# Layer-1 mixer of a graph transformer kernel: chunks of two tiles, with the feed-forward part of one chunk beside the attention of the next

## The chip, the cores and the metric

The kernel runs on one core of a Trainium2 chip. The metric is the device time of one execution in microseconds, the median of three runs. A core has five engines that run their own instruction streams in order: TensorE (PE in the profile; PEld is its weight load), VectorE (DVE), ScalarE (ACT), GpSimd (POOL) and SyncE (SP). They wait for one another by semaphores.

## The reference

Two layers on 3125 nodes with 256 features. Each adds a graph part and a mixer part, and then a feed-forward part with experts. The change touches only the place where layer 1 computes its graph part and its mixer:

```python
xn = _layernorm(x, axis=-1)
x = x + _L1_gnn_ref(xn, edge_index, ...) + _L1_mix_ref(xn[None], ...)[0]

# _L1_gnn_ref: graph attention over 50000 edges, 2 heads of 128
Wh = (x @ W_w + W_b).reshape(N, H, D)
e = leaky_relu(s[src] + t[dst])
ex = exp(e - segment_max(e, src)[src])
agg = segment_sum(ex / denom[src] * Wh[dst], src)

# _L1_mix_ref: linear attention with 8 heads of 32, then a feed-forward part of width 1024
q_phi, k_phi = _phi(x @ Wq + bq), _phi(x @ Wk + bk)
kv = einsum('blhd,blhe->bhde', k_phi, v);  k_sum = k_phi.sum(axis=1)
z = 1.0 / (einsum('blhd,bhd->blh', q_phi, k_sum) + 1e-06)
out = einsum('blhd,bhde,blh->blhe', q_phi, kv, z) @ Wo + bo
x = _layernorm(x + out, ln1_g, ln1_b)
ff = relu(x @ W1 + b1) @ W2 + b2
x = _layernorm(x + ff, ln2_g, ln2_b)
```

## The kernel before

The nodes lie in 25 tiles of 125 rows. `program` (L2983) runs one stage after another, each a `Block` with an instruction stream per engine, and a barrier of all engines stands between two stages. The change touches one stage, `sums_and_mix1` (L2577). Two streams of work without data in common run side by side in it.

The **edge stream** is the weighted sum over the edges. There are 25 groups of 16 columns. For a group t, POOL gathers 16 times 128 rows of `wh_dram` into one of four buffers `he_buf` (L2616); a buffer is free for group t+4 when the DMA that stores group t into `he_result` has landed (SP, L2634). DVE makes the exponents (`logits`, from L2777) and sets `e_ready`; ACT takes the exponential (`weights`, L2700) and multiplies each of the 16 columns in place (`weigh`, L2708, two instructions a column); DVE adds each column to the one after it (L2801 to L2819, 15 long instructions in a chain), copies the last (L2825), and sets `summed`, upon which SP stores the group.

The **mixer stream** is the attention and the feed-forward part. It first makes the key tables of all nodes (`keys_tensor`, `keys_scalar`, `keys_vector`), and then goes through the nodes in six chunks of four tiles (500 columns) and a last one of one tile. In a chunk each step needs the one before it:

- PE: query product (L2648, banks 0 and 1); ACT: positive and negative part and exponential (L2720 to L2724), sets `q_phi`.
- PE: `kv` and `ks` products (L2655 to L2658, banks 2, 3, 0, 1), sets `o_made`; DVE: `attention`, which adds, takes the reciprocal (L2857) and multiplies (L2860), sets `o_ready`.
- PE: output product for each tile (L2664 to L2667: bias row, residual through the identity, two of `wo`; banks 4 to 7), sets `o_made2`; DVE: sums of the first layer norm (L2836 to L2841), sets `var1`; ACT: square root (L2744), sets `std1`; DVE: normalization (L2845, L2848) into `y`, sets `y_ready`.
- PE: eight transposes (L2672, banks 0 and 1); ACT: scale and shift into `yT` (L2729), sets `y_moved`.
- PE: up product, eight blocks f of 128 hidden features (L2679, banks 0 to 3); ACT: relu of each (L2714), sets `acted`; PE: down product for each tile (L2685 to L2690, banks 4 to 7), sets `f_made` per tile; DVE: sums of the second layer norm; ACT: square root (L2761); DVE: normalization, times `norm2`, plus `norm2`, added to `X` (L2872 to L2877).

Nothing schedules this: the order of each stream is written out by hand. DVE's order in a chunk is `logits(t+1)`, `sums(t)`, `attention`, `logits(t+2)`, the first half of `sums(t+1)`, `after_attention`, the rest of `sums(t+1)`, `logits` and `sums` of the next two groups, `after_feed_forward`. ACT puts the relus between the columns of `weigh(t+3)`. PE has nothing but the mixer, one chunk behind the other. The room of the hidden features `hT` also holds the queries and the attention output (`qr`, `ql`, `oT`), and the tables of the keys before them. Where a name in the trace is `m_hT`, it is one of these.

## Time and profile before

| | us |
|---|---|
| median of three runs | 3766.0 (3750.4 to 3766.4) |
| the profiled execution | 3773.5 |
| its span, first to last instruction | 3771.8 |
| of it the stretch from the first `logits` to the last addition into `X` | 642.7 |
| PE busy in the whole span | 2309.4 |
| DVE busy in the whole span | 1909.2 |
| ACT busy in the whole span | 1335.4 |
| POOL busy in the whole span | 1332.4 |

No engine is busy for most of the span, since the stages have different limits. What a change in one stage is worth is read from that stage: from who waits for whom in it, and from the instructions in order of time. In the rows below, times are microseconds from the start of the span unless they are marked ns. An `x` with a number is a count of records; a matrix product in 32-bit floats leaves two records, one transpose leaves one. "DVEq" or "ACTq" as the releaser is a semaphore set by that engine's queue after a drain.

### The profile page before, as it was taken

The numbers are of one execution on the slowest core, as the hardware profiler recorded it, in microseconds if no ns is written. First come the engines' busy times: TensorE is split into PE (matmuls) and PEld (weight loads), VectorE is DVE, ScalarE is ACT, GpSimd is POOL, SyncE is SP. The second block draws the span as 40 slices with busy tenths as digits, with TensorE's granted clock in tenths as the row PEclk, the third lists the DMA queues.
The fourth block names the chain that finished last, engine by engine and source line by source line (L and its number), as shares of the span: only waits on it lengthen the run. The fifth ranks groups of instructions, "written<-read, shape, count | busy, mean of one in ns | idle before, by whom it ended". The sixth has DMA issues, their size and how long they took to land. (4 is left out here: it accounts for less than half of the span.)

```text
span 3771.8 us, 45605 instructions
## 1 busy us (share of the span) xinstructions
PE 2309.4 (61%) x13864; PEld 1628.2 (43%) x13864; DVE 1909.2 (51%) x4471; ACT 1335.4 (35%) x2931; POOL 1332.4 (35%) x1276
## 2 busy tenths in 40 slices
PE   3577645554499984761001756767660168999996
PEld 3352332444366653530000533434340146888874
DVE  5889825577411119894478456666654531111112
ACT  3369623564321112592000145555540111222221
POOL 0000014000177778774230377666605032000033
PEclk9899877776599995996555867777775579999998
DMA  1220021200222221310320445555522214455532
GB/s 57 76 90 0 9 51 27 96 1 0 39 52 69 42 49 44 111 7 5 135 76 11 98 126 187 166 180 176 175 102 63 66 42 139 178 192 188 181 114 74
DMA packets 166239, 329.42 MB, mean 87 GB/s; under 512 B 68140, under 2 KB 126812, under 8 KB 157940
## 3 DMA queue, kind: packets, MB, share of 16 engines
q0 software_dynamic: 66656, 153.23, 14.6%
q1 hardware_dynamic: 98944, 162.06, 12.8%
q10 hardware_dynamic: 520, 12.80, 0.8%
q8 instruction: 43, 0.70, 0.1%
q14 instruction: 76, 0.62, 0.1%
HBM read 220.15 MB, written 107.51 MB: 87 GB/s over the span
## 5 line engine op out<-in xcount | busy, mean ns | idle before, releaser
L1634 POOL DMA_INDIRECT ge_near<-gat_src,s_other x512 | 539.1, 1053 | 163.3 <-issue 163.3
L2616 POOL DMA_INDIRECT he_buf<-wh_dram,s_other x400 | 388.6, 972 | 187.3 <-issue 119.9
L177 PE MATMUL bank<-ident,XN 125*128 125x125 f32 x250 | 54.6, 348 | 442.2 <-DVE XN L276 400.8
L2270 ACT ACTIVATE x_hT<-bank,x_w 128x256 f32<-128x256 f32 x256 | 121.2, 473 | 373.1 <-PE bank L2247 373.1
L2708 ACT ACTIVATE he_buf<-he_buf,he_e 128x128 f32<-128x128 f32 x800 | 238.3, 388 | 2.8 <-issue 0.4
L177 PEld LDWEIGHTS bank<-ident,XN 125*128 125x128 f32 x250 | 42.4, 195 | 451.6 <-DVE XN L276 402.5
L2247 PE MATMUL bank<-x_xT,x_w 128*128 128x256 f32 x1024 | 229.1, 383 | 8.2 <-DMA x_w<-in_L_ffn_packed,x_rows 8.2
L2256 PE MATMUL bank<-x_w,x_hT 128*128 128x256 f32 x1024 | 229.4, 383 | 6.8 <-ACT x_hT L2270 6.7
L367 POOL DMA_INDIRECT g_near<-xt_dram,g_idx x25 | 30.4, 1217 | 516.9 <-DMA g_idx<-in_first_src 509.6
L2247 PEld LDWEIGHTS bank<-x_xT,x_w 128*128 128x128 f32 x1024 | 196.8, 192 | 35.3 <-issue 8.5
L1938 DVE TENSOR_TENSOR XN<-bank,arena 125x256 f32 (+1 forms) x100 | 42.5, 425 | 334.3 <-PE bank L1911 334.3
L2256 PEld LDWEIGHTS bank<-x_w,x_hT 128*128 128x128 f32 x1024 | 192.3, 190 | 38.9 <-issue 13.1
L2819 DVE SCALAR_TENSOR_TENSOR he_buf<-he_buf,he_cont 128x256 f32<-128x256 f32 x375 | 182.7, 487 | 35.3 <-ACT he_buf L2708 7.1
L1911 PE MATMUL bank<-arena 128*125 128x256 f32 x800 | 180.0, 383 | 21.6 <-ACT arena L1924 21.6
L1904 PE MATMUL bank<-XT,arena 128*128 (+1 forms) x448 | 174.7, 543 | 24.1 <-DMA arena<-in_L_ffn_b 24.1
L2209 POOL DMA_INDIRECT x_w<-in_L_ffn_packed,x_rows x32 | 30.1, 939 | 438.3 <-DVEq L2293 426.8
L1924 ACT ACTIVATE arena<-bank,arena 128x500 f32<-128x500 f32 (+1 forms) x112 | 70.9, 633 | 307.7 <-PE bank L1904 306.7
L1911 PEld LDWEIGHTS bank<-arena 128*125 128x125 f32 x800 | 147.9, 188 | 62.5 <-issue 29.6
L1203 ACT ACTIVATE s_far<-row,s_ki 128x512 f16<-128x512 f16 x256 | 157.0, 707 | 10.7 <-DVE s_nsr L1039 6.7
L1169 PE MATMUL bank<-XN 128*128 128x512 f16 (+1 forms) x488 | 118.0, 365 | 51.5 <-DVE XN L1053 51.5
L2282 DVE COPY x_xT<-bank 128x512 f32<-128x512 f32 x32 | 22.1, 692 | 229.6 <-PE bank L2237 229.6
L2679 PE MATMUL bank<-XT,m_w 128*128 128x500 f32 (+1 forms) x224 | 103.4, 629 | 50.9 <-ACTq L2731 50.9
(670 smaller groups left out, 5823.5 us busy)
## 6 DMA issues: line engine op xcount, KB each, us to landing
he_result<-he_buf SPq DMA_DIRECT2D x25, 2080.0 KB, 6.7
XN<-s_a_dram SPq DMA_DIRECT2D x57, 512.0 KB
x_y<-XN SPq DMA_DIRECT2D x24, 500.0 KB
x_x<-zero SPq DMA_DIRECT2D x1, 8192.0 KB, 26.9
ge_near<-gat_src,s_other POOLq DMA_INDIRECT x512
x_xs<-x_x SPq DMA_DIRECT2D x32, 256.0 KB, 8.8
x_y<-x_ys SPq DMA_DIRECT2D x32, 256.0 KB
he_buf<-wh_dram,s_other POOLq DMA_INDIRECT x400, 2.8
```

The source lines that it names most:

```text
L1169: pe.matmul(near, self.oav[j % 2][:, 8 * h + c, :], self.rv[2 * (j % 2) + h][:, c, :], start=False, stop=False)
L1203: last = act.activation(self.far[:, 4 * h + c, :], self.m.row16[:, 0:self.cols], ACT.Sign, bias=bias[:, bass.ds(u * BC + 8 * h + 4 + c, 1)])
L1634: pool.indirect_dma_start(out=G[:, c, :], out_offset=None, in_=m.gat_src, in_offset=bass.IndirectOffsetOnAxis(ap=ed.other[:, c:c + 1], axis=0)
L1904: last = pe.matmul(m.ps[f % 4][:, 0:nt * P], w.w1[e][:, k, f * 128:(f + 1) * 128], m.XT[:, bass.ds(c * CH + k * N, nt * P)], start=k == 0, ...
L1911: last = pe.matmul(m.ps[4 + j % 2][:P, 0:D], self.hT[:, f, j * P:(j + 1) * P], w.w2[e][:, f, :], start=f == 0, stop=f == FC - 1)
L2247: last = pe.matmul(m.ps[f % 4][:, 0:TS], w1[j][:, k, f * 128:(f + 1) * 128], xT[j][:, k, :], start=k == 0, stop=k == K2 - 1)
L2256: last = pe.matmul(m.ps[4 + s][:, 0:D], hT[j][:, f, s * 128:(s + 1) * 128], w2[j][:, f, :], start=f == 0, stop=f == FC - 1)
L2270: act.activation(hT[j][:, f, :], m.ps[f % 4][:, 0:TS], ACT.Gelu, bias=w[j][:, OB1 + f:OB1 + f + 1]).then_inc(acted, 1)
L2616: pool.indirect_dma_start(out=buf[j][:, c, 0:HF + H], out_offset=None, in_=m.wh_dram, in_offset=bass.IndirectOffsetOnAxis(ap=ed.other[:, t ...
L2679: done = pe.matmul(m.ps[f % 4][:, 0:w], x.w1[:, k, f * 128:(f + 1) * 128], yT(c, w)[:, k, :], start=k == 0, stop=k == K2 - 1)
L2708: done = act.activation(f, f, ACT.Copy, scale=e[j][:, c, h:h + 1])
L2819: dve.scalar_tensor_tensor(v[:, c, 0:HF], v[:, c - 1, 0:HF], spread.cont[:, t * BC + c:t * BC + c + 1], v[:, c, 0:HF], ALU.mult, ALU.add)
```

## The change

The mixer goes in chunks of two tiles (`CT = 2`, 250 columns), twelve of them and a last one of one tile. The attention of chunk c, the feed-forward part of chunk c-1 and the second layer norm of chunk c-2 are written beside one another. Two halves of 250 columns share a bank: queries in bank 0, `ks` and `kv` products in 1 and 2, transposes in 3, up products in 4 and 5, output product in 6 and down product in 7. `hT`, `qr`, `ql` and `oT` get room of their own inside `m1_room`, and there are two `y` (`y1`, `y2`) and two sets of the norm's small tiles. A semaphore `f_read` tells PE that bank 7 has been read. The number of edge groups, their buffers and the streams of POOL and SP stay as they are.

```diff
+    CT = 2
+    CW = CT * P
+    LAST = NT // CT
@@ tensor
-                for c in range(NCH + 1):
-                    (queries, values, output, turn, up, down of chunk c)
+                queries(0)
+                pe.wait_ge(x.kv_ready, 1)
+                for c in range(LAST + 1):
+                    values(c)
+                    output(c)
+                    if c:
+                        up(c - 1)
+                        down(c - 1)
+                    if c < LAST:
+                        queries(c + 1)
+                    turn(c)
+                up(LAST)
+                down(LAST)
@@ scalar
+                def hidden(c):
+                    w = width(c)
                     act.wait_ge(S["y_turned"], c + 1)
...
                     act.drain().then_inc(S["y_moved"], 1)
+                    for f in range(FC):
+                        if f % 2 == 0:
+                            act.wait_ge(S["up"], c * FC + f + 2)
+                        act.activation(hT[:, f, 0:w], two(m.ps[4 + f // 2 % 2], w)[:, f % 2, :], ACT.Relu,
+                                       bias=x.b1[:, f:f + 1]).then_inc(S["acted"], 1)
+                for c in range(LAST):
+                    t = c * CT
+                    if c >= 2:
+                        root(c - 2, 1)
+                    weigh(t)
+                    if c:
+                        hidden(c - 1)
+                    root(c, 0)
+                    weigh(t + 1)
+                    queries(c + 1)
+                root(LAST - 2, 1)
+                hidden(LAST - 1)
+                root(LAST, 0)
+                root(LAST - 1, 1)
+                hidden(LAST)
+                weigh(LAST * CT)
+                root(LAST, 1)
@@ vector
+                for c in range(LAST):
+                    t = c * CT
+                    logits(t)
+                    if c >= 2:
+                        after_feed_forward(c - 2)
+                    attention(c)
+                    sums(t)
+                    spread_of(c, 0)
+                    logits(t + 1)
+                    after_attention(c)
+                    sums(t + 1)
+                    if c:
+                        spread_of(c - 1, 1)
+                after_feed_forward(LAST - 2)
+                attention(LAST)
+                spread_of(LAST, 0)
+                after_attention(LAST)
+                spread_of(LAST - 1, 1)
+                after_feed_forward(LAST - 1)
+                logits(LAST * CT)
+                sums(LAST * CT)
+                spread_of(LAST, 1)
+                after_feed_forward(LAST)
```

The line in brackets stands for the text of the loop before, which is printed above. `spread_of` makes the sums of a layer norm (0 the first, 1 the second) and sets `var0` or `var1`; `root` is ACT's square root for it and sets `std0` or `std1`; `after_attention` and `after_feed_forward` begin with the wait for it; `weigh` now holds the exponential too.

PE, around the up product, before. The names: `m_wo` the output weights, `m_y` the normalized rows, `m_w` the up or down weights, `m_hT` the room of the hidden features:

```order
L2667 MATMUL bank<-m_wo,m_hT 125x256 x2
L2672 MATMUL bank<-ident,m_y 128x125 x8
L2679 MATMUL bank<-XT,m_w 128x500 x16
L2685 MATMUL bank<-m_rows,ones 125x256
L2687 MATMUL bank<-ident,XT 125x128 x2
L2690 MATMUL bank<-m_w,m_hT 125x256 x8
```

The same place now, from the second half of the `kv` and `ks` products to the transposes (`m_wq` are the query weights, `m_room` the shared room):

```order
L2659 MATMUL bank<-m_room,m_ks 128x250
L2660 MATMUL bank<-m_room,m_ks 128x250
L2667 MATMUL bank<-m_rows,ones 125x256
L2668 MATMUL bank<-XN,ident 125x256
L2670 MATMUL bank<-m_wo,m_room 125x256 x2
L2667 MATMUL bank<-m_rows,ones 125x256
L2668 MATMUL bank<-XN,ident 125x256
L2670 MATMUL bank<-m_wo,m_room 125x256 x2
L2687 MATMUL bank<-XT,m_w 128x250 x16
```

Before, the transposes of a chunk stood between its output product and its up product. Now the up product that follows an output product is that of the chunk before, and the transposes come after the down product and the next queries.

ACT, around the relus, before (`he_e` the exponents, `he_buf` the gathered rows, `m_rs` the variances, `m_s,m_g` shift and scale of the first layer norm):

```order
L2744 ACT_TABLE_LOAD
L2744 ACTIVATE m_rs<-m_rs 125x4
L2700 ACT_TABLE_LOAD
L2700 ACTIVATE he_e<-he_e 128x34
L2708 ACTIVATE he_buf<-he_buf,he_e 128x128 x32
L2729 ACTIVATE XT<-bank,m_s,m_g 128x500 x2
L2714 ACTIVATE m_hT<-bank,m_b 128x500 x2
L2700 ACTIVATE he_e<-he_e 128x34
L2708 ACTIVATE he_buf<-he_buf,he_e 128x128 x8
L2714 ACTIVATE m_hT<-bank,m_b 128x500 x2
```

The same place now, one half of the work for a chunk:

```order
L2747 ACTIVATE XT<-bank,m_s,m_g 128x250 x2
L2753 ACTIVATE m_room<-bank,m_b 128x250 x8
L2759 ACT_TABLE_LOAD
L2759 ACTIVATE m_rs<-m_rs 125x2
L2725 ACT_TABLE_LOAD
L2725 ACTIVATE he_e<-he_e 128x34
L2730 ACTIVATE he_buf<-he_buf,he_e 128x128 x32
L2737 ACTIVATE m_room<-bank,m_nbq 128x250 x2
```

The relus no longer stand between columns of a `weigh`: all eight come first, then the square root of the next chunk's first layer norm with a table load, then a second table load and the whole `weigh`. Such loads stand four times in every chunk of two tiles; before, they stood four times in every chunk of four.

## Rows read from the trace of the kernel before

**Rows 1.** The page, its first line: the whole span.

```profile
span 3771.8 us, 45605 instructions
```

**Rows 2.** Stretches: length, then busy PE, PEld, DVE, ACT, POOL, clock, DMA, GB/s.

```profile
2193.90:2836.70 642.80, 416.73 (x1184) 245.18 (x1184) 399.13 (x1035) 335.62 (x966) 368.52 (x379) 0.73 0.49 162
...
2427.00:2443.00 16.00, 15.94 (x32) 9.23 (x32) 6.42 (x23) 0.00 (x0) 12.34 (x13) 0.50 0.41 106
2458.00:2475.00 17.00, 16.48 (x32) 7.08 (x32) 14.17 (x40) 11.05 (x33) 12.08 (x12) 0.83 0.65 227
```

**Rows 3.** Waits, 2195 to 2838: waiter <- releaser, total, times, longest.

```profile
ACT m_rs L2744 <- DVE m_rs L2841: 182.3, 7, 27.2
...
PE bank L2664 <- DVEq L2861: 102.7, 7, 26.2
...
PE bank L2679 <- ACTq L2731: 50.9, 7, 8.6
```

**Rows 4.** Groups by shape, 2195 to 2838: busy, mean ns | idle before, releasers.

```profile
L2616 POOL DMA_INDIRECT he_buf<-wh_dram,s_other x378 | 367.6, 972 | 180.1 <-issue 112.7 <-DMA he_result<-he_buf 67.4
...
L2857 DVE RECIPROCAL m_hT<-m_hT 128x1000 f32<-128x1000 f32 x6 | 38.4, 6403 | 0.4
...
L2714 ACT ACTIVATE m_hT<-bank,m_b 128x500 f32<-128x500 f32 x48 | 30.2, 667 | 34.3 <-PE bank L2679 34.3
L2848 DVE TENSOR_SCALAR m_y<-bank,m_mv,m_rs 125x256 f32<-125x256 f32 x50 | 23.9, 537 | 1.1
L2836 DVE BATCH_NORM_STATS2 m_st<-bank 125x6 f32<-125x256 f32 x50 | 19.8, 426 | 161.0 <-PE bank L2690 106.6 <-PE bank L2667 54.3
...
L2872 DVE TENSOR_TENSOR m_y<-m_y,m_norm 125x1024 f32<-125x1024 f32 x6 | 7.4, 1229 | 0.4
...
L2857 DVE RECIPROCAL m_hT<-m_hT 128x250 f32<-128x250 f32 x1 | 1.7, 1718 | 0.1
```

**Rows 5.** In order of time, DVE, 2407 to 2430: start, duration, instruction.

```profile
2407.43 0.29 DVE L2801 TENSOR_SCALAR he_e<-he_e,he_cont 128x2 f32<-128x2 f32 x1
...
2417.90 1.26 DVE L2855 TENSOR_SCALAR m_hT<-bank 128x500 f32<-128x500 f32 x2
...
2427.10 0.19 DVE L2777 TENSOR_TENSOR he_e<-he_buf,he_ke 128x32 f32<-128x32 f32 x1
...
2429.24 0.29 DVE L2801 TENSOR_SCALAR he_e<-he_e,he_cont 128x2 f32<-128x2 f32 x1
```

**Rows 6.** In order of time, PE, up and down product of one chunk.

```profile
2458.24 16.48 PE L2679 MATMUL bank<-XT,m_w 128*128 128x500 f32 x32 [8.28 <-ACTq L2731]
...
2477.30 5.30 PE L2690 MATMUL bank<-m_w,m_hT 128*125 128x256 f32 x16
...
2483.69 3.62 PE L2690 MATMUL bank<-m_w,m_hT 128*125 128x256 f32 x16
...
2488.40 3.62 PE L2690 MATMUL bank<-m_w,m_hT 128*125 128x256 f32 x16
```

**Rows 7.** In order of time, ACT, 2407 to 2448: columns, table loads, exponential.

```profile
2407.70 9.45 ACT L2708 ACTIVATE he_buf<-he_buf,he_e 128x128 f32<-128x128 f32 x32
...
2417.18 1.28 ACT L2744 ACT_TABLE_LOAD   x1
...
2445.78 1.28 ACT L2700 ACT_TABLE_LOAD   x1
...
2447.07 0.23 ACT L2700 ACTIVATE he_e<-he_e 128x34 f32<-128x34 f32 x1
```

**Rows 8.** In order of time, DVE: first logits, third group's logits, last addition.

```profile
2193.93 0.19 DVE L2777 TENSOR_TENSOR he_e<-he_buf,he_ke 128x32 f32<-128x32 f32 x1
...
2231.61 0.19 DVE L2777 TENSOR_TENSOR he_e<-he_buf,he_ke 128x32 f32<-128x32 f32 x1 [0.28 <-DMA he_buf<-wh_dram,s_other]
...
2836.20 0.43 DVE L2877 TENSOR_TENSOR X<-m_y,X 125x256 f32<-125x256 f32 x1
```

**Rows 9.** DMA issues, 2190 to 2860: count, KB each, us to landing.

```profile
he_result<-he_buf SPq DMA_DIRECT2D x25, 2080.0 KB, 6.7
```

More of the change, by code:

```diff
@@ L2457 @@
     HD = 32
+    WORDS = 3720
     def __init__(self, m, hT):
@@ new lines, in queries, with values @@
+                            done = pe.matmul(two(m.ps[0], width(c))[:, o, :], x.wq[:, k, o * 128:(o + 1) * 128], yT(c)[:, k, :],
+                                             start=k == 0, stop=k == K2 - 1)
+                    done.then_inc(S["q_made"], 1)
+                def values(c):
+                    w = width(c)
+                    pe.wait_ge(S["q_phi"], c + 1)
+                    for bank, table in ((m.ps[2], x.kv), (m.ps[1], x.ks)):
+                        for o in range(K2):
+                            pe.matmul(two(bank, w)[:, o, :], table[:, o, :], qr[:, o, 0:w], start=True, stop=False)
+                            done = pe.matmul(two(bank, w)[:, o, :], table[:, o, :], ql[:, o, 0:w], start=False, stop=True)
@@ L2701, in weights @@
                     act.drain().then_inc(e_exp, 1)
-                def weigh(t, columns):
-                    j = t % R
-                    for c in columns:
+                    for c in range(BC):
                         for h in range(H):
@@ L2823, in last_sums @@
-                def last_sums(t):
-                    row_sums(t, range(BC // 2, BC))
-                    dve.tensor_copy(last[:, 0:HF + H], buf[t % R][:, BC - 1, 0:HF + H])
+                    for c in range(1, BC):
+                        dve.drain()
+                        dve.wait_ge(weighted, t * BC + c + 1)
+                        dve.scalar_tensor_tensor(v[:, c, 0:HF], v[:, c - 1, 0:HF], spread.cont[:, lo + c:lo + c + 1],
+                                                 v[:, c, 0:HF], ALU.mult, ALU.add)
@@ L2878, in after_feed_forward @@
                     dve.drain()
[L2879 to L2897 removed]
+                dve.memset(last[:, 0:HF + H], 0.0)
```

224 lines of the change are left out of this document (81 added, 143 removed).

## The prediction

> **What bounds the kernel now.** I read the page's first line, then the stage's busy times as one stretch, then who waits for whom in it, the groups by shape, and one chunk in order of time. The stage takes 642.8 us of a span of 3771.8 [rows 1, 2]. In it PE is busy for 416.7, DVE for 399.1, POOL for 368.5 and ACT for 335.6, so no engine fills it: the reader is to see two thirds on each at best. The waits tell why. In its seven chunks ACT sits 182.3 us in front of the square root of a layer norm until DVE has the sums, PE sits 102.7 us before the output product until DVE has divided the attention, and 50.9 us before the up product [rows 3]. DVE in turn waits 161.0 us before the sums of its layer norms, 106.6 of it for the down product [rows 4]. They wait in a ring: a chunk's steps follow one another, and each engine stands in order behind a step of the same chunk. PE pays twice. After its waits it works at the lower of its two levels: the output product of one chunk ran 16 us at a granted clock of 0.50, thus 1.2 GHz, and in the 17 us of an up product the mean was 0.83, which is 1.2 GHz for about a third of them, 5.8 us, and 2.4 GHz for the rest [rows 2].
>
> **The change, part by part.** The steps of one chunk are spread over three rounds, so that each engine has older work while a step is made. I work out how long a round of two tiles takes, then the beginning and the end.
>
> *DVE's work in a round.* `logits` took 2429.24 - 2427.10 = 2.1 us and `sums` of one group 2417.90 - 2407.43 = 10.5 [rows 5]. `attention` for 500 columns took 2427.10 - 2417.90 = 9.2, mostly its reciprocal; between 6.40 us at 1000 elements and 1.72 at 250 [rows 4] half the columns give 3.3 for the reciprocal, and 4.8 in all. Normalizing two tiles is 2 x 0.54 plus a small reciprocal and a drain, 1.3. The three passes of the second norm are 1.23 for 1024 elements, 0.7 for 512 with a gap, so `after_feed_forward` is 1.3 + 2.3 = 3.6. The sums of a norm are 2 x 0.43 and small ones, 1.4 [rows 4]. A round is 2.1 + 3.6 + 4.8 + 10.5 + 1.4 + 2.1 + 1.3 + 10.5 + 1.4 = 37.7 us: the work per tile is what it was.
>
> *POOL's work* is unchanged: 367.6 busy and 112.7 of issue for 378 gathers, 1.27 us each [rows 4], 40.7 for the 32 of a round. Its 67.4 us of waits for stores came from DVE's bunched sums; now two `sums` come evenly, and a buffer has three more gathers, 61 us, to come free.
>
> *The path through a round.* Count from the start of `logits(2c)`. DVE has the attention divided at 2.1 + 3.6 + 4.8 = 10.5. PE had the `kv` products early (queries stand at the end of the round before) and has been idle some 7 us, as it was before each output product of the trace; so I take that product at 1.2 GHz, as it ran there: 16 us for four tiles [rows 2], 8.0 for two, to 18.5. The relus' input `yT` is ready at about 14 (weigh 9.8 us, then 1), and does not count. The up product comes next in PE's row. At 2.4 GHz it takes half of 17 x 0.83, less idle, 6.8; with 5.8 us at half speed, as in the trace, 9.7, to 28.2 (16.48 us for 500 columns [rows 6]). The last pair of relus adds 1.0 (0.67 each at 500 columns [rows 4]), to 29.2. Here the change adds a wait: in ACT's row stand behind the relus a table load, the root, a second load, and the whole `weigh` of the second group; and DVE, which was at `after_attention` at 2.1 + 10.5 + 1.4 + 10.5 = 24.5, stands there with `sums` of the second group queued behind. Load 1.3 and root 0.2 [rows 7] bring it to 30.7, a stall of about 6 us that the trace of before did not have in this form. The second load and the exponential, 1.6 us, run beside DVE's normalization of 1.3. From the exponential on, at 32.2, `sums` takes its 10.5, to 42.7, and the sums of the second norm 1.4: **44.0 us a round**. ACT's 16 columns end at 32.2 + 9.5 = 41.7, and the queries' activations, about 2.2, at 43.9, in time. The down product ends at 29.2 + 11.1 = 40.3: the first tile 6.4 and each other 4.7 apart [rows 6]; queries at 42. POOL (40.7) and DVE (37.7) both fit in 44.
>
> *Costed at nothing:* 22 more table loads, of which two a round are in the path above and two lie where ACT would wait anyway (DVE's `attention` covers them); twice as many weight loads per up column (7.08 us of load beside 16.48 of product [rows 2], so still under the product at half the width); `f_read`, set long before. If the cover for the loads went, each costs 1.3.
>
> *Beginning.* The first `logits` stay at 2193.9. Round 0 has no second norm and no relus: 35 us. Round 1 waits for the third group, which lands at 2231.6 [rows 8] because POOL sets that, and has no second norm either: 44.0 - 3.6 = 40.4, to 2272.0. The ten rounds after it: 440, to 2712.
>
> *End.* It is serial, and this is the change's own cost. `after_feed_forward(10)` 4.9 with its wait, attention of one tile 2.8, its output product 4.0, `up(11)` 9.7, relus 1.0, `down(11)` 11.1, sums 1.4, root 0.3, `after_feed_forward(11)` 3.4, `logits` 2.1, and the last group's `sums` 10.6: 51.3. Then the last store, 6.7 us to landing [rows 9], which lay under the last chunk's feed-forward before, now sets the end: 58.0. The stage ends at 2712 + 58 = 2770 instead of 2836.6 [rows 8]: **66.6 us less**. The profiled execution took 3773.5, so 3707; the median of the runs is 7.5 below that execution, so **3699 us**.
>
> **A rule that speaks against it.** The loads of the trace follow the column before within 0.03 us (2417.15, 2417.18), and the exponential begins 1.29 us after the load before it [rows 7]: a switch costs 1.28 and nothing more.
> The Trainium skill, "ScalarE: Activation LUTs", section "What ACT_TABLE_LOAD costs", says that a switch to another set costs about 1283 ns for the load and about 1380 ns of drain, 2.66 us. The trace agrees with the first and shows no drain of that length. By the page the 22 loads on the path would add 22 x 1.38 = 30 us, and the time would be 3729.
>
> **The rivals.** (1) *PE keeps 2.4 GHz through output and up product.* For it: values, queries and transposes now fill gaps that were idle. The output product then takes about half, -4.0, and the up product -2.9: a path of 37.1, and POOL's 40.7 sets the round. The last round would start at 2231.6 + 10 x 40.7 = 2638.6, end 37.9 later, and the tail be 8 shorter: 2726.5, 110 us less, **3656**. Against it: an idle stretch of 7 us before the output product remains, and in the trace a product of 16 us after such a wait never rose.
> (2) *Slower: PE stays at 1.2 GHz the whole round.* Its work in ten rounds would be in the path: 10.5 + 8.0 + 13.6 (up) + 1.0 + 18.8 (down, twice 4.7 x 2) + 3.4 (queries) + 2.2 (ACT) = 57.5, and the end some 20 longer: 10 x 13.5 + 20 = 155 later than forecast, 88 slower than now, **3854**. It decides from a round of (2836.6 - 58 - 2272) / 10 = 50.7 us. Products of 250 columns with gaps around them speak for it; that each up product of the trace did rise speaks against.
> (3) *The lag buys little, PE rises late.* With the whole up product at 1.2 GHz (+3.9) the round is 47.9, 39 later: **3738**. PE's row then also has its queries done at 46, close behind. For it: the up product now has an output product at 1.2 GHz directly ahead instead of transposes and idle time.
> (4) *A table switch costs more than the load* where it follows relus or square roots. Two are on the path of ten rounds and two in the tail. With a second load's time as the bound [rows 7], 22 x 1.28 = 28 us, **3727**. Against it: the rows on columns and exponential just given.
>
> **How the numbers follow.** Forecast 0.60 (own range 3682 to 3720: 42.5 to 46 us a round); rival 1 0.15; rival 2 0.08; rival 3 0.13; rival 4 0.04. The time is the forecast's, 3699. The range takes rival 1 at its price and reaches to rivals 4 and 3: 3654 to 3738, leaving out rival 2 and the outer parts of 1 and 3. Half a per cent, about what a measurement can tell from no change here, is 19 us: faster than 3747 are the forecast, rivals 1 and 4 and most of 3, 0.87 with a margin for a miss of mine in the order; within 0.5% 0.05; slower 0.08.
>
> **What would show each step.** Right: the stage ends near 2770; the distance between two `attention` reciprocals is 44; DVE idles 5 to 7 us before the reciprocal of the first norm, released by ACT's root; the output product has a clock of 0.50 and the up product a mean near 0.7; the gathers wait for no store after the first rounds; the wait before the root is small. Rival 1: clock 1.00 there, and DVE waiting for gathers. Rival 2: PE busy without gaps at 0.50. Rival 3: DVE waiting some 10 us. Rival 4: a gap around each table load. Wrong altogether, if DVE waits in front of `attention` or `sums` for something else.

## The result, and the profile after

The changed kernel takes 3671.8 us (median of four runs, 3669.5 to 3681.8) where the kernel before takes 3762.3 (four runs, 3750.4 to 3766.4): a ratio of 0.977, 95% interval 0.974 to 0.980. That is 90 us less where 67 were forecast, and 27 us under the forecast of 3699. Ratios here and below are of a kernel's fast runs alone, which matters for one variant, the root among the relus, whose ten runs scatter by 100 us. The profiled execution took 3670.6 us. In the stage only three things moved: the rounds are 1.6 us shorter than forecast, the beginning 1.4 longer, the end 1.0 shorter.

First the page of after, its first line and the group of the stage's gathers (against [rows 1] and the first row of [rows 4]):

```profile
span 3668.8 us, 46561 instructions
...
L2622 POOL DMA_INDIRECT he_buf<-wh_dram,s_other x400 | 393.4, 984 | 122.5 <-issue 122.5
```

POOL waits for no store any more; before, 67.4 us of its idle time ended with `he_result`.

Stretches of after, in the columns of [rows 2]: the stage up to the next stage's first work, its ten full rounds, then an output product and the up product behind it.

```profile
2179.40:2739.90 560.50, 402.81 (x1520) 309.57 (x1520) 408.11 (x1081) 385.25 (x1088) 372.84 (x379) 0.81 0.56 185
2258.93:2682.97 424.04, 316.76 (x1203) 243.13 (x1204) 325.46 (x861) 311.52 (x871) 312.19 (x317) 0.84 0.61 200
2396.90:2404.40 7.50, 7.47 (x16) 4.65 (x17) 6.46 (x17) 2.68 (x9) 5.67 (x7) 0.50 0.34 94
2404.40:2412.00 7.60, 7.44 (x34) 6.32 (x32) 5.35 (x21) 2.61 (x7) 5.77 (x7) 0.96 0.75 272
```

Ten rounds take 424.0 us, 42.4 each; 44.0 were forecast. The work is what it was (DVE 408 us busy against 399 before, POOL 373 against 369) but for ACT, which has 385 against 336; it lies in 560 us instead of 643.

The waits of after, 2195 to 2770, in the form of [rows 3]:

```profile
ACT m_room L2753 <- PE bank L2687: 138.9, 52, 11.9
...
PE bank L2667 <- DVEq L2862: 75.6, 12, 7.5
DVE m_rs L2847 <- ACT m_rs L2759: 56.5, 15, 7.3
...
ACT m_rs L2759 <- DVE m_rs L2842: 20.6, 3, 10.8
```

ACT's 182.3 us before the root are 20.6. What took their place: ACT waits for the up product in front of the relus, and DVE waits for the root, the two places at which the path of a round crosses engines.

One round in order of time, start, duration, instruction (an X addition ends the chunk of two rounds ago):

```profile
2386.20 0.18 DVE L2789 TENSOR_TENSOR he_e<-he_buf,he_ke 128x32 f32<-128x32 f32 x1
...
2391.30 0.69 DVE L2876 TENSOR_TENSOR X<-m_y,X 125x512 f32<-125x512 f32 x1
...
2392.81 3.28 DVE L2859 RECIPROCAL m_room<-m_room 128x500 f32<-128x500 f32 x1
...
2396.93 1.21 PE L2667 MATMUL bank<-m_rows,ones 1*125 1x256 f32 x2 [7.16 <-DVEq L2862]
...
2404.78 7.06 PE L2687 MATMUL bank<-XT,m_w 128*128 128x250 f32 x32
...
2411.88 0.83 ACT L2753 ACTIVATE m_room<-bank,m_b 128x250 f32<-128x250 f32 x2 [0.86 <-PE bank L2687]
2412.72 1.28 ACT L2759 ACT_TABLE_LOAD   x1
...
2414.02 0.20 ACT L2759 ACTIVATE m_rs<-m_rs 125x2 f32<-125x2 f32 x1
2414.24 1.28 ACT L2725 ACT_TABLE_LOAD   x1
2414.26 0.17 DVE L2847 RECIPROCAL m_rs<-m_rs 125x2 f32<-125x2 f32 x1 [3.46 <-ACT m_rs L2759]
...
2417.35 8.50 DVE L2827 SCALAR_TENSOR_TENSOR he_buf<-he_buf,he_cont 128x256 f32<-128x256 f32 x15
...
2427.57 0.18 DVE L2789 TENSOR_TENSOR he_e<-he_buf,he_ke 128x32 f32<-128x32 f32 x1
```

Read it as the forecast counted, from the first row: attention divided at 10.6 (forecast 10.5), output product done at 18.6 (18.5), up product at 25.6 (28.2), relus at 26.5 (29.2), root at 28.0 (30.7), next round at 41.4 (44.0). In this round the whole error lies in one step, the up product. It is the shortest one of the trace; their mean is given further down.

The end of the stage, against the last row of [rows 8]:

```profile
2732.50 0.32 SPq L2640 DMA_DIRECT2D he_result<-he_buf  x1
...
2735.64 0.43 DVE L2876 TENSOR_TENSOR X<-m_y,X 125x256 f32<-125x256 f32 x1
...
2739.97 0.29 DVE L1373 TENSOR_SCALAR hc_dg<-ident,s_key 128x128 f32<-128x128 f32 x1 [3.66 <-PEq L73]
```

The next stage starts 7.5 us after the last store is issued and only 4 after the last addition: the store sets the end, as forecast. In the kernel before the same first instruction waited 1.0 us at the barrier, and began at 2837.87.

**Where the 103 us between the two spans (3771.8 and 3668.8) are.** The stage with its barrier went from 2193.93 to 2837.87, 643.9, to 2179.38 to 2739.97, 560.6: 83.3 us. Ahead of the stage nothing is changed, but it begins 14.5 us earlier. The 512 gathers of an earlier stage explain that; their line (count, shortest, median and longest in ns, first and last start) in the trace of before, and then of after:

```profile
L1634 POOL DMA_INDIRECT ge_near<-gat_src,s_other x512: 940/944/25159, 1018.4 to 1758.5; - x171
```

```profile
L1634 POOL DMA_INDIRECT ge_near<-gat_src,s_other x512: 941/947/2347, 1017.3 to 1742.5; - x171
```

One gather of before took 25 us, and none of after took over 2.4, so that the row of gathers is 740.1 us long in the one and 725.2 in the other. Other kernels' traces have such a gather too (21.4 and 17.6 us in two variants below), so the 14.5 us are not the change's. Behind the stage 5.1 us are left over (933.9 against 928.8), in small pieces: 2.1 of them ahead of the products L2935 (L2943 in after), the rest spread over the products behind; PE is busy for 678.2 us there instead of 681.2. Their cause is open. That leaves 83 us for the change by the traces and 90 by the medians.

### The profile page after: what moved, and what is told of

Read it like the earlier page. It is cut to its first block and busy times, and to the rows that moved or that the text cites. A ratio compares the mean times of both kernels' runs of the same rounds, so it can differ in the third digit from the quotient of the medians.

```text
span 3668.8 us, 46561 instructions
## 1 busy us (share of the span) xinstructions
PE 2295.4 (63%) x14200; PEld 1693.0 (46%) x14200; DVE 1918.7 (52%) x4517; ACT 1384.9 (38%) x3055; POOL 1323.2 (36%) x1276
## 5 line engine op out<-in xcount | busy, mean ns | idle before, releaser
L1634 POOL DMA_INDIRECT ge_near<-gat_src,s_other x512 | 524.5, 1024 | 163.1 <-issue 163.1
L177 PEld LDWEIGHTS bank<-ident,XN 125*128 125x128 f32 x250 | 40.7, 189 | 452.4 <-DVE XN L276 402.6
L1911 PE MATMUL bank<-arena 128*125 128x256 f32 x800 | 180.0, 382 | 21.6 <-ACT arena L1924 21.6
L1911 PEld LDWEIGHTS bank<-arena 128*125 128x125 f32 x800 | 147.9, 188 | 62.6 <-issue 29.6
L1203 ACT ACTIVATE s_far<-row,s_ki 128x512 f16<-128x512 f16 x256 | 157.0, 710 | 10.5 <-DVE s_nsr L1039 6.7
L2291 DVE TENSOR_TENSOR x_ys<-bank,x_w 128x256 f32<-128x256 f32 x64 | 27.2, 425 | 207.7 <-PE bank L2256 207.7
```

What stands on the lines that cost most here:

```text
L177: last = pe.transpose(m.ps[j][:, k * P:(k + 1) * P], m.XN[:, bass.ds(t * D + k * 128, 128)], m.ident[:P, :P])
L1203: last = act.activation(self.far[:, 4 * h + c, :], self.m.row16[:, 0:self.cols], ACT.Sign, bias=bias[:, bass.ds(u * BC + 8 * h + 4 + c, 1)])
L1634: pool.indirect_dma_start(out=G[:, c, :], out_offset=None, in_=m.gat_src, in_offset=bass.IndirectOffsetOnAxis(ap=ed.other[:, c:c + 1], axis=0)
L1911: last = pe.matmul(m.ps[4 + j % 2][:P, 0:D], self.hT[:, f, j * P:(j + 1) * P], w.w2[e][:, f, :], start=f == 0, stop=f == FC - 1)
```

## The experiments

The runs fell on several chips. On some of them the kernel before itself takes 4617 us instead of 3760, so each variant is compared with the kernel before on its own chip, and ratios are compared between chips of the same kind. I call the two kinds the 3760 chips and the 4617 chips.

| variant | chip kind | us | before, us | ratio (95%) |
|---|---|---|---|---|
| changed kernel | 3760 | 3671.8 | 3762.3 | 0.977 (0.974 to 0.980) |
| kernel before again | 4617 | 4618.8 (one run) | 4616.8 | - |
| changed kernel again | 4617 | 4488.9 | 4617.9 | 0.9727 (0.9711 to 0.9743) |
| no lag | 4617 | 4557.7 | 4617.9 | 0.9870 (0.9854 to 0.9887) |
| no lag, another chip | 4617 | 4549.8 | 4618.4 | 0.9857 (0.9841 to 0.9873) |
| second norm one round earlier | 4617 | 4506.7 | 4616.8 | 0.9764 (0.9748 to 0.9781) |
| filler ahead of the output product | 4617 | 4491.3 | 4617.9 | 0.9721 (0.9705 to 0.9738) |
| filler in the kernel before | 4617 | 4616.0 | 4616.8 | 0.9998 (0.9987 to 1.0008) |
| root among the relus | 4617 | 4621.8 (ten runs, 4543 to 4644) | 4616.8 | 0.9912 (0.9863 to 0.9961), three of the ten |
| other tail | 4617 | 4471.7 | 4617.9 | 0.9689 (0.9673 to 0.9705) |
| root among the relus, other tail | 4617 | 4585.5 | 4618.4 | 0.9927 (0.9894 to 0.9961) |
| filler, other tail | 3760 | 3654.8 | 3756.3 | 0.9723 (0.9704 to 0.9743) |
| few gathers | 3760 | 3672.9 (one run) | 3756.3 | - |

I begin with the two on a 3760 chip, the kind for which the forecast was made.

### Does POOL set the round?

```diff
-                    for c in range(BC):
+                    for c in range(BC if t < R else 2):
...
-                    dve.wait_ge(rows[j], 16 * BC * (t // R + 1))
+                    dve.wait_ge(rows[j], 16 * (BC + 2 * (t // R)))
```

> The changed kernel with 2 of the 16 gathers of each tile in this stage after the fourth tile, the other 14 left out (14 of 16 blocks of those tiles are not loaded; all operations on them still run). It takes away POOL's work and most of the loads. On a chip where the kernel before takes 3762 us: theory A (the chain over TensorE sets the round, POOL's 41.3 us does not) says rounds stay at 42 to 42.5 us, 3665 to 3680; rival B (POOL's supply of rows sets it) says rounds of 38 us or less, 3625 or less. On a chip where the kernel before takes 4617 us: theory C (there the engines get no instructions at times while POOL's gathers run) says rounds fall from 56 to 42 to 44 us, 4350 to 4380; rival D (something else, such as the clock or the stores, makes rounds of 56 us there) says they stay over 50 us, 4430 or more.

The variant leaves out 14 of the 16 gathers of every group from the fifth on and keeps all the work on their rows. It took 3672.9 us (one run) against 3671.8 with all gathers, and the ten rounds had a mean of 42.2 us against 42.4. In this variant (columns of [rows 2], ten rounds; then POOL's longest wait in the stage):

```profile
2225.10:2646.80 421.70, 317.85 (x1200) 243.79 (x1200) 322.43 (x860) 310.76 (x868) 49.49 (x51) 0.84 0.30 119
...
POOL he_buf L2622 <- DMA he_result<-he_buf: 343.7, 19, 20.2
```

POOL works 49 us of 422 and the round is the same. So theory A holds: with everything else as it is, POOL's supply does not set the round, though at 32 x 1.29 = 41.3 us it is only 1.1 us from doing so. Most of the stage's loads are gone with the gathers (DMA share 0.30 instead of 0.61), so the load on the DMA engines does not set it either.

### Is the clock of the output product worth what rival 1 said?

```diff
+                def fill():
+                    for i in range(7):
+                        pe.matmul(m.ps[0][:, 0:500], x.w1[:, 0, 0:128], x.w1[:, 1, 0:500], start=True, stop=True)
...
                     values(c)
+                    if c:
+                        fill()
                     output(c)
```

with the other order of the tail (shown below) in the same kernel.

> The changed kernel with both edits: seven products of 500 columns into a bank that nobody reads, ahead of the output product of every round but the first, and the tail in another order (the last tile's logits, weights and sums ahead of the last feed-forward parts). Theory A (the rounds are the chain over TensorE, attention divided to sums, until something else is next): with the output product at 2.4 GHz the chain is shorter by some 4 us, and POOL's 32 gathers at 0.98 + 0.31 = 1.29 us each, 41.3 us a round, come next, so that the rounds fall from 42.4 to 41.3 where the kernel before takes 3762 us: 11 us less, and 10 to 17 from the tail, 3645 to 3650. Rival B (the chain alone, POOL has slack through its four buffers): rounds of 38.5 to 39.5, 3620 to 3630. Rival C (the clock changes nothing): the tail's 10 to 17 us alone, 3655 to 3662. On a chip where the kernel before takes 4617 us, the same as the tail alone in all theories: 4465 to 4480, ratio 0.967 to 0.970.

3654.8 us, a ratio of 0.9723 where the changed kernel had 0.977: some 18 us less than the changed kernel. Three stretches of its trace tell what the filler did (columns of [rows 2]): an output product that came straight behind the filler, one that came 1.67 us after it, and the up product behind the first.

```profile
2396.30:2400.40 4.10, 4.10 (x17) 2.81 (x17) 3.57 (x11) 2.36 (x8) 3.19 (x4) 1.00 0.44 114
2355.20:2362.50 7.30, 7.25 (x16) 4.76 (x17) 6.24 (x17) 2.33 (x7) 5.78 (x6) 0.55 0.41 111
2400.40:2407.40 7.00, 6.97 (x34) 5.93 (x32) 5.98 (x15) 2.49 (x6) 5.34 (x6) 1.00 0.38 106
```

PE's own rows (the last bracket of the first is the gap):

```profile
2355.25 0.69 PE L2667 MATMUL bank<-m_rows,ones 1*125 1x256 f32 x2 [1.67 <-DVEq L2867]
2355.87 1.22 PE L2668 MATMUL bank<-XN,ident 125*125 125x256 f32 x2
...
2390.37 6.03 PE L2706 MATMUL bank<-m_w 128*128 128x500 f32 x14
2396.33 0.69 PE L2667 MATMUL bank<-m_rows,ones 1*125 1x256 f32 x2
2396.95 0.70 PE L2668 MATMUL bank<-XN,ident 125*125 125x256 f32 x2
```

Six us of filler at 2.4 GHz did not carry the clock over the gap of 1.67 us: the second pair of products is back at 1.22 us. Without a gap everything stays at 2.4 GHz, the output product takes 4.1 us instead of 8.0, and three of the five rounds with such an output product came to 37.7 to 38.7 us, near the 37.1 of rival 1's path. But they did not stay that short. DVE's waits in this kernel, 2195 to 2685:

```profile
DVE he_e L2794 <- DMA he_buf<-wh_dram,s_other: 23.5, 4, 8.4
DVE m_rs L2852 <- ACT m_rs L2764: 19.5, 6, 4.0
```

After a round of 37.7 came one of 46.8, in which DVE stood 8.3 us until gathered rows landed. The ten rounds had a mean of 41.0, which is POOL's 41.2 for 32 gathers (312.8 us busy for 319 gathers in those rounds, and 0.31 of issue for each). So by the rounds theory A holds: POOL is next, little more than 1 us behind the path. The time alone, 5 us above theory A's range and next to rival C's, would not have told them apart. By the trace the ten rounds are 15.4 us shorter, but the round ahead of them is 4.7 longer and the one behind them 4.0 longer (distances of reciprocals 41.9 and 44.3 against 37.2 and 40.3), which leaves 6.7; the tail gives 7.9, and 2.9 lie ahead of the first reciprocal, where nothing shows their cause: 17.5 in the stage. Of the 4.0 behind, 2.1 are the last group's `logits`, which the other order of the tail puts there; with them the filler gives 8.8 and the tail 5.8.

The filler alone, on a 4617 chip:

> The changed kernel with seven products of 500 columns on constant weights into bank 0, which nobody reads, between values and output product of each round from the second on (5.9 us at 2.4 GHz). It computes nothing new. They fill the 7 us in which PE idles there. Theory (the clock falls in that idle time, and the output product at 1.2 GHz is on the path): output product at clock 1.00 in about 4 us instead of 8, up product 7, DVE's wait for the first root from 4.4 us to under 1; the round then goes to the gathers' pace of 40.7 from 42.5: 15 to 25 us faster than the changed kernel. Rival (the output product stays at 0.50 whatever stands before it, as it did for 16 us in the kernel before): output still 8 us, time within 5 us of the changed kernel, or slower by what the filler delays.

It brought nothing there (0.9721 against 0.9727), as the rival had it for the time, although the output product is at full clock, as the theory had it and the rival not (a granted clock of 1.00 in eleven of the twelve rounds). PE in one round of it:

```profile
3131.25 6.03 PE L2706 MATMUL bank<-m_w 128*128 128x500 f32 x14
...
3139.32 0.69 PE L2667 MATMUL bank<-m_rows,ones 1*125 1x256 f32 x2
...
3141.34 3.54 PE L2687 MATMUL bank<-XT,m_w 128*128 128x250 f32 x16
3155.45 6.48 PE L2687 MATMUL bank<-XT,m_w 128*128 128x250 f32 x16 [10.56 <-ACT m_room L2758]
```

The 4 us gained are followed by a wait of 10.6 in the middle of the up product, on an ACT that had stopped. This kind of stop is the subject of the last section. The same filler in the kernel before (14 products ahead of the output product and 8 ahead of the up product):

> The kernel before, in its old order, with filler products on constant weights into bank 4 while PE waits: fourteen of 500 columns before the output product and eight before the up product of each chunk but the first and last (the last has none). It tells the clock's part in the time of before from the ring's. Theory (the ring of waits is the main thing, the clock makes PE's part of it longer): output product 9 us instead of 16 and up product 13.5 instead of 16.5, 10 us less in each of five or six chunks: 40 to 60 us faster than before, and still slower than the changed kernel by 30 to 50. Rival (the clock explains the whole gain of the change): as fast as the changed kernel, 3670. Rival (output products never rise): under 20 us faster.

The four tiles' output product fell from 16 to about 8.5 us (in four of the five chunks that have the filler) and the up product from 16.4 to 13.7, and the distance of two chunks stayed at 141 us (140 without), the time at 0.9998. On a 4617 chip the clock is not what is late. Whether it would have paid on a 3760 chip was not tried.

### Is it the lag or the smaller chunk?

In PE's stream, and likewise in ACT's and DVE's:

```diff
-                    if c:
-                        up(c - 1)
-                        down(c - 1)
+                    turn(c)
+                    up(c)
+                    down(c)
                     if c < LAST:
                         queries(c + 1)
-                    turn(c)
-                up(LAST)
-                down(LAST)
```

> The changed kernel with its chunks of two tiles, banks and rooms, but without the lag: PE makes values, output, turns, up and down of one chunk and then the next queries; ACT and DVE follow. Theory (the lag is what gains): a round is then attention 7, output 8, norm and turns 5, up 9, down 11, norm, up to 60 us and more against 49 per two tiles before; 12 rounds of 60 to 64: the kernel is at 3850 to 3920 us, slower than before. Rival (the smaller chunk itself gains, since each wait is half as long): 3680 to 3760 us.

> The changed kernel without its lag: chunks of two tiles, but attention, feed-forward part and LN2 of a chunk one behind the other in the same round, as the kernel before does with four tiles. Theory A (the lag is what takes the chain apart): without it a round is attention divided to sums 10.5, output product 8, sums and turn 3, up product with its relus 9 to 10, down 8 to 9, the sums behind it 10.5, queries and values 10, by the rows of after, 58 to 62 us, and the time is 3672 + 10 to 12 times 16 to 20 = 3840 to 3910, slower than before. Rival B (the smaller chunk is what helps, the lag little; where the kernel before takes 4617 us, the lag was worth only 5.4 us a round): rounds of 47 to 50 us, 3730 to 3765. On a chip where the kernel before takes 4617 us: rounds of 61 us, 4550 to 4565.

Both runs fell on 4617 chips, on two different ones, and agree: rounds of 61.5 us, ratios of 0.987 and 0.986. That the round lies where theory A put it is no support for it, since theory A spoke of a 3760 chip; on these chips the kernel before needs 140 us for four tiles, thus 70 for two, and not the 49 of a 3760 chip (98 to 99 for four), and the changed kernel 56. Rounds of 70 (before), 61.5 (chunks of two, no lag) and 56 (with the lag) would give the smaller chunk 8.5 us for two tiles and the lag 5.5. The whole kernel says otherwise, 60 us for the smaller chunk (4617.9 to 4557.7) and 69 for the lag (to 4488.9), because the beginning and the end count too.

For a 3760 chip the last full round of these traces tells more. By then POOL's gathers are over, and the stops of unnamed cause, which are the subject of the last section, are gone with them. The last gather and the last two `attention` reciprocals of the variant without lag:

```profile
3507.01 0.95 POOL L2622 DMA_INDIRECT he_buf<-wh_dram,s_other  x1 [0.30 <-issue]
...
3527.89 3.28 DVE L2851 RECIPROCAL m_room<-m_room 128x500 f32<-128x500 f32 x1
...
3579.57 1.72 DVE L2851 RECIPROCAL m_room<-m_room 128x250 f32<-128x250 f32 x1
```

The same distance is 39.9 us in the changed kernel on a 4617 chip and 40.3 on a 3760 chip, and 95.8 and 96.1 in the kernel before: here the two kinds of chips agree. So 51.7 us without lag (52.1 in the other run) stand against 48 for two tiles before and 40.3 with the lag. Without the stops the smaller chunk alone makes a round about 4 us longer, and the lag takes 11 to 12 off it: in this round the whole gain is the lag's. That is theory A in kind and not in size: with the 2 us by which an ordinary round of the changed kernel is longer than its last (42.4 against 40.3) a round without lag would be about 54 us, an estimate, between its 58 to 62 and rival B's 47 to 50. It rests on one round in each of two traces; no variant without lag ran on a 3760 chip.

The changed kernel on such a chip, for comparison:

> The changed kernel once more, as the yardstick for the variants of this chip. Theory (the lag breaks the ring of waits): 3660 to 3685 us. Its rounds, the distance between two attention reciprocals, should again be 42 to 43 us, and the up product of a round should alternate between about 7 and 8.6 us. If the 90 us were an accident of one chip, the ratio would leave 0.97 to 0.98.

Its ratio stayed within 0.97 to 0.98; its rounds, 54.6 to 59.6 us, and its time did not come out as expected, since it ran on the other kind of chip.

The second norm one round earlier, so that its lag is one chunk instead of two:

```diff
-                    if c >= 2:
-                        root(c - 2, 1)
...
+                    if c:
+                        root(c - 1, 1)
...
-                    if c >= 2:
-                        after_feed_forward(c - 2)
...
+                    if c:
+                        after_feed_forward(c - 1)
```

> The changed kernel with one of the two lags undone: the second norm of chunk c-1 is finished at the end of the same round, not in the next. Theory: DVE then waits at the end of each round for ACT, which has columns and queries to finish before the root: 1.5 to 3 us a round, 18 to 36 us slower than the changed kernel, still 50 us or more faster than before. Rival (both lags carry the gain alike): about half of the gain gone, 45 us slower than the changed kernel.

The ratio is 0.9764 against 0.9727, 17 us slower, at the low end of what was expected; the two were measured on two chips of the 4617 kind. Spread over twelve rounds that would be 1.5 us each, but the two profiled executions are only 4.7 us apart and their rounds 56.2 and 56.7 us in the mean. So the second lag is worth little beside the first; how much is not settled.

### Can DVE's wait for the root be taken out, and the tail be shortened?

The root and the exponential between the relus, so that `after_attention` and `sums` can begin earlier:

```diff
                     if c:
-                        hidden(c - 1)
-                    root(c, 0)
-                    weigh(t + 1)
+                        hidden(c - 1, {4: lambda: root(c, 0), 6: lambda: weights(t + 1)})
+                    else:
+                        root(c, 0)
+                        weights(t + 1)
+                    weigh(t + 1, False)
```

> The changed kernel with ACT's order changed in a round: the root of the first norm stands between the second and third pair of relus, the exponential of the round's second group between the third and fourth pair, so that both table loads fall into the 0.86 us gaps in which ACT waits for the up product. Theory (the path of a round runs through relus, load, root, load, exponential, columns): the columns of the second group begin 2 us earlier, DVE's wait for the root goes from 4.4 us to about 1 to 2, and the round from 42.5 to about 40.7, where the gathers set it: 12 to 20 us faster than the changed kernel. Rival (the path is PE's: output, up, down, queries): no difference over 3 us, or slower because the last relus and the down product come later.

> The changed kernel with the root of the attention's normalization and the weights' exponential put between the third and fourth pair of relus, instead of behind all of them, and the tail in the other order. Theory A (DVE's stall for the root, 4.4 us in the mean, is part of the chain, beside the up product; POOL's 41.3 us a round are next): rounds fall from 42.4 to 40.5 to 41.5 us where the kernel before takes 3762 us, and with 10 to 17 us of the tail 3640 to 3655. Rival B (the chain goes through TensorE's up and down products and the stall is slack): rounds stay at 42 to 42.5, the tail alone, 3655 to 3662. Rival C (the two table loads among the relus hold the up product's banks, and TensorE waits longer): rounds of 43 to 45, 3665 to 3690. On a chip where the kernel before takes 4617 us: 4500 to 4620, as the move of the root alone did there.

Both are slower than the changed kernel on 4617 chips (0.991 and 0.993 against 0.973 without), and the first scatters by 100 us between runs; by the median of all ten it is no faster than the kernel before. The first has rounds of 54 to 57 us, like the changed kernel, until it falls into a rhythm of 75; the second has 68 to 75 from the start. ACT in one of these, in the second kernel, and POOL at its end:

```profile
3202.05 9.45 ACT L2735 ACTIVATE he_buf<-he_buf,he_e 128x128 f32<-128x128 f32 x32
3245.97 0.83 ACT L2742 ACTIVATE m_room<-bank,m_nbq 128x250 f32<-128x250 f32 x2 [34.47 <-remote]
...
3240.04 0.95 POOL L2622 DMA_INDIRECT he_buf<-wh_dram,s_other  x1 [0.31 <-issue]
3275.76 0.94 POOL L2622 DMA_INDIRECT he_buf<-wh_dram,s_other  x1 [34.78 <-DMA he_result<-he_buf]
```

ACT does nothing for 34 us while POOL issues the last 23 of a row of 32 gathers, and goes on 5 us after the last of them; then POOL waits 35 us for the stores that depend on ACT. So what was measured is how the order meets these stops, and not the question that was asked. Whether 4 us of DVE's wait can be had on a 3760 chip stays open.

The tail, with the last group's `logits`, weights and `sums` ahead of the last feed-forward parts (ACT's part; DVE's `logits(LAST * CT)` and `sums(LAST * CT)` move likewise, ahead of `after_feed_forward(LAST - 2)` and behind `attention(LAST)`):

```diff
                 root(LAST - 2, 1)
+                weigh(LAST * CT)
                 hidden(LAST - 1)
                 root(LAST, 0)
-                root(LAST - 1, 1)
                 hidden(LAST)
-                weigh(LAST * CT)
+                root(LAST - 1, 1)
                 root(LAST, 1)
```

> The changed kernel with the last edge group taken ahead at the end: logits and sums of group 24 before the last chunk's norm instead of behind the feed-forward part of chunk 11, its weighting before the relus of chunk 11, and the relus of the last chunk before the root of chunk 11. Theory (the tail of 56 us is serial, its end is set by the last sums and the last store): DVE's idle 4, 7 and 9 us take in the 12.6 us of the group and the store lies under the products: 9 to 13 us faster than the changed kernel. Rival (the tail is a chain of PE's products, and the group's work was beside it): within 3 us.

This one pays: 0.9689 against 0.9727, measured on the same chip, 17 us by the medians. Not all of that is the tail's. In the two profiled executions the stretch from the last reciprocal of `attention` to the next stage's first work is 43.6 us instead of 51.8, while 8.6 us lie ahead of the stage, where the kernels do not differ. In the filler kernel on a 3760 chip the same stretch is 44.1 us instead of 52.0 (2680.47 to 2724.57 against 2687.93 to 2739.97), and 1.0 us at the barrier instead of 3.7. So the stretch is 8 us shorter on both kinds, and 6 to 7 with the `logits` that now stand ahead of it; 9 to 13 were expected. It does no extra work, so of all variants it is the one to keep; alone it was not run on a 3760 chip.

## Why the prediction was right where it was

**The bound: a ring of steps, not an engine.** Right, and that it is the lag that opens it is shown by the round of 51.7 us without it. The work of PE, DVE and POOL hardly changed, ACT's grew by 50 us, and PE, DVE, ACT and POOL are each busy for two thirds to three quarters of a stage that is 83 us shorter. The run with few gathers shows it for POOL directly.

**DVE's 37.7 us of work in a round.** Right: in the round shown DVE idles 3.5 + 0.3 us of 41.4, so it works 37.6.

**The path.** Each step held to 0.2 us but one. *Mis-sized: the up product.* The forecast had 6.8 us at 2.4 GHz and 5.8 of the product's time at half speed, 9.7 in all, the second figure carried over from the up product of four tiles. The twelve up products of two tiles took 7.06 to 8.64 us, 7.9 in the mean, and those at full clock throughout in the filler kernel 6.9. So the slow part adds 0.1 to 1.7 us, not 2.9. In the kernel before PE came to the up product from an idle stretch [rows 6], and 16 us of output product at 1.2 GHz had not raised it [rows 2]; now the up product follows the output product without a gap, and the clock rises in its first 3 us or so (0.1 to 1.7 us more are 0.2 to 3.4 us at half speed). The forecast saw the new neighbour and gave it to rival 3, as a reason for a *later* rise. It was the other way round: 1.8 us too much in a product and 1.6 in a round, 16 in ten, which with the beginning and the end is all of the difference in the stage (576.1 us forecast, 560.6 measured). The variants without lag bear the reading out: their up products of the same 250 columns come after transposes and a gap of 1.1 us, and 22 of them took 8.5 to 10.0 us, 9.0 in the mean, at a granted clock of 0.70 to 0.82, where the changed kernel's had 0.80 to 0.98. These ran on 4617 chips, so it is a strong hint and not a clean comparison.

**DVE's wait for the root.** Right in kind and place, too long in size for the same reason: about 6 us forecast, 3.5 to 5.1 measured, 4.4 in the mean.

**POOL.** Right: no wait for stores, and 41.3 us a round (40.7 forecast) just under the path. That it is so close was told by rival 1, and the filler kernel then ran into it.

**Costed at nothing.** Right: the weight loads stayed under the product, 6.32 us beside 7.44 in the up product shown above; the stage has 48 table loads instead of 25, and they cost their 1.28 us where they stand in the path.

**Beginning and end.** From the first `logits` to the third round 79.5 us (78.1 forecast). The end took 57.0 (58.0), with the exposed store, but that it fits so well is luck. `up(11)` took 7.5 us (9.7 forecast) and `down(11)` 9.5 (11.1), and two things made up for it: the last group's `sums` waited 2.8 us for its exponential, which stands in ACT's row behind the relus of the last chunk and which the forecast had at nothing, and the barrier came 7.5 us after the store (6.7).

**Rival 1** (all at 2.4 GHz, POOL sets 40.7) did not happen by itself: the output product ran at a granted clock of 0.50 in every round. With the filler it happened in part, 41.0 a round. **Rival 2** would have been 50.7 us or more; it was 42.4. **Rival 3** wanted 47.9. **Rival 4**, a switch that costs more than its load: in the round shown the last relu ends at 2412.71, the load begins at 2412.72 and takes 1.28, the root begins at 2414.02, and the second load follows it at 2414.24. There is no gap, with twice as many loads as before.
The Trainium skill, "ScalarE: Activation LUTs", section "What ACT_TABLE_LOAD costs", adds about 1380 ns of drain to each switch; these rows leave room for 0.02 us.

**The rest of the 27 us** between forecast and median, some 12, is not in the stage. The forecast subtracted from a profiled execution that began the stage at 2193.9, when three others on such chips begin it at 2179 to 2182; correcting it by the 7.5 us between that execution and the median took back only half. The 7.0 us that are left and the 5.1 behind the stage are the 12, and neither is the change's by anything that the traces show.

## What to carry to other kernels

Where every engine is busy for two thirds and the waits form a ring, spread the steps of a chunk over rounds; cutting the chunk alone did not shorten the round where nothing else disturbed it. Sum the path of one round step by step; that sum was good to 4% here, and it tells which engine is next (POOL, 1.1 us behind) before one spends work on the clock. Compare the sum with the trace step by step in the end of the loop as well, where two errors can cancel. Do not carry the slow part of a product over from a trace in which it began after idle time: ask what runs directly ahead of it now. Look at the tail of a pipelined loop for work that waits for nothing, since 6 to 8 us lay in a few moved calls.

## What the runs showed of the hardware

**Two kinds of chips.** The same kernel before has medians of 3756 to 3766 us on the one kind and 4617 to 4618 on three chips of the other, and its single runs lie within half a per cent of them. The difference is there only where POOL issues gathers: set side by side, instruction by instruction, the two traces of the kernel before are within 6 us of each other up to the 512 gathers of the earlier stage, have parted by 607 us at the first `logits`, part by another 240 in the stage of the change, and are within 2 us of each other behind it. The kernel before was run again to see whether these gathers vary by themselves from 1053 to 1024 ns in the mean; it fell on such a chip and had 1008. On 3760 chips the traces of two variants, with the same code there, have 1049 and 1044, so they do vary by themselves. The first row is the products L1911 of the earlier stage with the 512 gathers in the kernel before on a 3760 chip, the second the same on a 4617 chip (busy, mean ns, idle before):

```profile
L1911 PE MATMUL bank<-arena 128*125 128x256 f32 x800 | 180.0, 383 | 21.6 <-ACT arena L1924 21.6
```

```profile
L1911 PE MATMUL bank<-arena 128*125 128x256 f32 x800 | 220.6, 439 | 626.5 <-issue 582.7
...
PE bank L1911 <- issue: 582.7, 16, 79.5
```

Sixteen stops, up to 79.5 us long, in which PE waits for nothing that the trace shows, while POOL's gathers run at full pace (1008 ns each, faster than on the 3760 chip). In the stage of the change they are shorter. The changed kernel there, ACT and PE, in one round:

```profile
3189.52 0.83 ACT L2753 ACTIVATE m_room<-bank,m_b 128x250 f32<-128x250 f32 x2 [7.73 <-PE bank L2687]
3197.00 1.55 ACT L2753 ACTIVATE m_room<-bank,m_b 128x250 f32<-128x250 f32 x4 [6.65 <-remote]
...
3216.97 0.27 PE L2677 MATMUL bank<-ident,m_y 125*128 125x125 f32 x1 [1.76 <-issue]
3219.77 0.37 PE L2677 MATMUL bank<-ident,m_y 125*128 125x125 f32 x1 [2.53 <-issue]
```

ACT's stop ended 2 us into a pause of POOL's gathers; PE's instructions came one at a time, some 2 us apart, and flowed again once the gathers paused at 3218. It looks as if the engines' instructions reach them late while gathers are under way on such a chip, and in the last full round, with the gathers over, all variants with chunks of two tiles are free of such stops. The Trainium skill, "Runtime: NRT & Kernel Launch", section "Instruction fetch mechanics", says that each sequencer fetches the next 16 KiB of its instructions over a DMA queue of its own and that this is mostly hidden; on the 3760 chips the trace agrees (21.6 us of idle time before L1911, none of it "issue"), on the others, if fetching is the cause, it is not hidden. That cause is argued and not shown: the kernel with few gathers, which would have told, fell on a 3760 chip. What is shown is that there a round of the changed kernel takes 56 us where it takes 42.4 here, and that a gain of 4 us on PE (the filler) or a move on ACT (the root) is swallowed or reversed by the stops, while the change itself keeps its ratio.

**The clock falls over a short gap.** After six us of dense products at 2.4 GHz a gap of 1.67 us was followed by products at 1.2 GHz (the rows of 2355 above), while the output product that followed without a gap stayed at 2.4. Behind a gap of 0.82 us (2640.25) it stayed at 2.4 too. I had expected the filler to be enough for every round; it was for five of the twelve.
